# Query/key norms through 32-column sums and one inverse root, and VectorE operations over two PSUM banks

## What is computed

```python
q = _causal_dwconv_silu(q_l + qd, q_conv_w).reshape(b, s, h, dh)
k = _causal_dwconv_silu(k_l + kd, k_conv_w).reshape(b, s, h, dh)
...
q, k = (_l2norm(q), _l2norm(k))     # x * rsqrt(sum(x * x) + 1e-6) over the 16 channels of a head
...
Sd = gt[..., None, None] * Sst                       # per token: decay the state,
kS = jnp.einsum('bhk,bhkv->bhv', kt, Sd)             # read it with the key,
Snew = Sd + jnp.einsum('bhk,bhv->bhkv', kt, bt[..., None] * (vt - kS))
ot = jnp.einsum('bhk,bhkv->bhv', qt, Snew)           # and again with the query
...
scores = jnp.einsum('bhqd,bhkd->bhqk', q * SCALE, k) # cross attention: softmax over 64 keys
```

## Time and profile before

| | us |
|---|---|
| time of three runs | median 1374.06 (1372.43 to 1379.7) |
| the profiled execution: its own time | 1380.29 |
| its span in the trace | 1378.5 |
| turn i = 0 / steady turns i = 1 to 6 / drain and last | from 47 / some 155 each from 202 on / from about 1120 and 1267 |

### The profile page before, as it was taken

One profiled execution on the slowest core, in us unless ns is written; L12 is line 12 of the kernel. 1 busy time (PEld: TensorE's weight loads), 2 busy tenths in 40 slices (PEclk: granted clock), 3 DMA queues, 4 the chain that ended last, 5 costly groups with the idle time before them and its releaser, 6 DMA issues.

```text
span 1378.5 us, 40816 instructions
## 1 busy us (share of the span) xinstructions
PE 1291.2 (94%) x17045; PEld 838.7 (61%) x17077; DVE 1139.6 (83%) x3060; ACT 907.6 (66%) x1760; POOL 206.8 (15%) x204
## 2 busy tenths in 40 slices
...
PEclk9999999999999999999999999999999999999999
...
DMA packets 22782, 35.77 MB, mean 26 GB/s; under 512 B 1992, under 2 KB 18504, under 8 KB 22344
## 3 DMA queue, kind: packets, MB, share of 16 engines
...
## 4 chain that ended last, share of the span: by engine, by line
PE 68%; DVE 16%; ACT 10%; issue 4%; DMA 1%; POOL 0%; SPq 0%; DVEq 0%; ACTq 0%
PE bank L2210 14%; PE four L1970 5%; PE bank L1884 5%; PE bank L1757 4%; PE bank L1782 4%; PE bank L2125 4%; PE bank L2103 3%; PE bank L2139 3%; PE four L1989 2%; PE four L1782 2%; PE bank L1886 2%; ACT L833 2%; PE bank L1811 2%; PE four L2014 2%; PE bank L1789 2%
## 5 line engine op out<-in xcount | busy, mean ns | idle before, releaser
L2210 PE MATMUL bank<-w_sb,cs 128*128 128x512 f32 x512 | 248.7, 602 | 2.9 <-ACT qkv L1109 0.4
L798 POOL TENSOR_TENSOR decayed<-state,pk 128x512 f32<-128x512 f32 x64 | 76.1, 1189 | 671.3 <-DVE state L1499 671.3
L2210 PEld LDWEIGHTS bank<-w_sb,cs 128*128 128x128 f32 x512 | 92.4, 189 | 95.8 <-issue 71.5
L1109 ACT ACTIVATE cs<-bank 128x512 f32<-128x512 f32 x112 | 66.9, 598 | 99.2 <-PE bank L1763 48.8
L833 ACT ACT_TABLE_LOAD x82 | 105.2, 1283 | 1.5
L1357 DVE SCALAR_TENSOR_TENSOR qkv<-pre,l_sb,qkv 128x512 f32<-128x512 f32 x144 | 101.6, 751 | 0.0
L1884 PE MATMUL bank<-hT,w_sb 128*128 128x512 f32 x192 | 95.2, 619 | 3.9 <-ACT hid L913 2.2
L1696 DVE SCALAR_TENSOR_TENSOR cs<-cs,rwt 128x256 f32<-128x256 f32 x196 | 88.2, 485 | 6.2 <-ACT cs L1109 2.8
L1045 ACT COPY cs<-bank 128x512 f32<-128x512 f32 x114 | 66.0, 579 | 41.3 <-PE bank L2125 41.2
L1582 DVE TENSOR_REDUCE pkc<-bank 128x8 f32<-128x512 f32 x116 | 74.3, 682 | 21.1 <-PE bank L2103 20.0
L1811 PEld LDWEIGHTS bank<-c_sb 128*128 128x128 f32 x588 | 74.6, 199 | 11.3 <-issue 10.3
...
## 6 DMA issues: line engine op xcount, KB each, us to landing
...
```

The source lines that it names most:

```text
L798: fin("dec", tt(decayed[:, :, :, :], state[:, :, :, :], eGC[:, c, :].unsqueeze(1).unsqueeze(3).to_broadcast([P, 4, G * B, DH]), ALU.mult))
L2210: mm(dst, x1T[:, k, b * TB:b * TB + TB], ew[:, k, ep * 512:ep * 512 + 512], start=k == 0, stop=False)
```

## The change

The norms: the four blocks of squares are kept in four buffers. One step `sum` makes four products with 32-column weights (`bones8`), each of which fills 32 partitions of the one bank 0, with eight head sums in four copies. One `rs` takes Ln and Exp over 128 x 512. A new step `rsp` spreads the roots by four products of 32 rows each (`wide8`) into banks 0 to 3; it waits for `rs`, and, since it overwrites what `grow` left, for `d_ready` (behind `gsub.1`) and both `egr` (behind `gexp.1` and `gexp.2`, which now wait for `d_ready` themselves). `norm` reads its factor from PSUM. `vturn` waits for two norms. On VectorE the paired operations of `max`, `zc`, `dsel`, `gsub`, the tap copies and the halo copies become one operation each over both halves, and `psub` is one signal a unit. All lists and the `KEEP` table are new. Cut to its core (the order lists are shown where the text speaks of them):

```diff
-DVE_IN, DVE_AB, DVE_CD, ACT_IN, ACT_AB, ACT_CD = 22, 64, 57, 2, 6, 18
+DVE_IN, DVE_AB, DVE_CD, ACT_IN, ACT_AB, ACT_CD = 19, 62, 49, 2, 3, 18
...
     "steady": {
         "pe": steps('''
+        -router.0 +gate.1 grow -turn2.0 sum +cond -qx.0.0 rsp -turn2.1 -qx.0.1 vturn -qx.1.0 -sc.0.0 -sc.0.1 -qx.1.1
+        raw.0 raw.1 -sc.1.0 -sc.1.1 -pt.0 raw.2 -pt.1 raw.3 raw.4 -pv.0 raw.5 raw.6 -pt.2 -sc.2.0 -sc.2.1 -pt.3 raw.7
...
+        cs.7.0 cs.7.1 -turn6.1 *rot co.0 co.1 -ffd.0 -ffd.1 onorm.0 *gate.0 onorm.1 wo.0 -ffu.0 -ffu.1 wo.1 wo.2'''),
         "dve": steps('''
+        -ln2.0.0 -ln2.0.1 dsel.0 dsel.1 gsub.0 gsub.1 -ln2.1.0 -ln2.1.1 norm.0 norm.1 norm.2.0 norm.3.0 norm.2.1
+        norm.3.1 -max.0.0 -max.0.1 -max.1.0 am.0 +cond -max.1.1 am.1 -av.0.0 am.2 -av.0.1 -max.2.0 -max.2.1 am.3
...
         "act": steps('''
+        sq.2 -moe.0 -moe.4 -ln2.0 -moe.18 +cond.0 sq.3 -turn2.0 +gate.1 rs gexp.2 gexp.1 -ln2.1 gexp.0 -turn2.1 -qx.0
...
     "drain": {
         "pe": steps('''
+        +proj.1.0 grow +proj.1.1 -turn2.0 -turn2.1 -qx.0.0 -qx.0.1 sum -qx.1.0 rsp -qx.1.1 -sc.0.0 vturn -sc.0.1 raw.0
...
         "act": steps('''
+        +proj.4 -ln2.0 -ln2.1 sq.2 -turn2.0 sq.3 -moe.14 -turn2.1 -qx.0 gexp.1 kx.0 gexp.2 -top.0 -route.0 *gate.0 rs
...
 # first(i), ScalarE
-                    if j >= 2:
-                        up("sum_ps", j - 1)
-                    fin("sq", A(osq[:, j % 2, :], qkv[:, j, :], ACT.Square))
+                    fin("sq", A(squares[j], qkv[:, j, :], ACT.Square))
+                def sum_():
                     log_exp()
+                    up("sum_ps")
+                    inv_sqrt(ch, squares[0], bank[0][:, :], eps6, 1.0, "rs")
...
                     else:
+                        up("d_ready")
                         g = k - 1
                         fin("egr", A(egr[:, 32 * g:32 * g + 32, :].rearrange("p n t -> p (n t)"), bank[2 + g][:, :], ACT.Exp))
...
 # first(i), VectorE
-                        for a, n in enumerate(pair):
-                            tap[a] = ch1.link(V.tensor_copy(pre[:, n % 4, :, 0:3], halo[:, n, :, :]))
+                        at = 2 * m % 4
+                        tap[0] = tap[1] = ch1.link(V.tensor_copy(pre[:, at:at + 2, :, 0:3], halo[:, 2 * m:2 * m + 2, :, :]))
...
-                        up("rs", j + 1)
-                    tmp = norms[:, 32 * (j % 2):32 * (j % 2) + 32, :]
+                        up("rsp_ps")
+                    tmp = v3(bank[j][:, :])
...
+                    ring = flat(zc_ring[:, c % 4, :, :, :].rearrange("p n x m -> p n (x m)")).rearrange("p (a n) -> p a n", a=2)
+                    fin("zc", stt(ring, four[:, 2:4, 0:D], C("x0"), C("zx").unsqueeze(1).to_broadcast([P, 2, D]), ALU.mult, ALU.add))
...
 # second(j), VectorE
-                        for a in range(2):
-                            up("sc_ps", 2 * u + a + 1)
-                            highest[a] = link(red(mx[:, a, :], sc[a], AX.X, ALU.max))
+                        up("sc_ps", 2 * u + 2)
+                        highest[0] = link(red(flat(mx), sc, AX.X, ALU.max))
...
+                    fin("psub", tt(prob_of(j, u).rearrange("p (h n) -> p h n", h=16), sc, bc(flat(mx), NK), ALU.subtract))
...
 # first(i), TensorE
-                    fin("sum_ps", mm(bank[j % 2][:, :], C("bones"), osq[:, j % 2, :], start=True, stop=True))
+                def sum_():
+                    up("sq", 4)
+                    if i:
+                        pe.wait_ge(ev["ors"].sem, ev["ors"].at(i - 1, 2))
+                    tiled()
+                    for j in range(4):
+                        last = mm(bank[0][32 * j:32 * j + 32, :], C("bones8"), squares[j], start=True, stop=True)
+                    fin("sum_ps", last)
+                def rsp():
+                    up("rs")
+                    up("d_ready")
+                    up("egr", 2)
+                    tiled()
+                    for j in range(4):
+                        rows_ = slice(32 * j, 32 * j + 32)
+                        last = mm(bank[j][:, :], C("wide8")[rows_, :], squares[0][rows_, :], start=True, stop=True)
+                    fin("rsp_ps", last)
                 def vturn():
                     up("bv")
-                    up("rs", 4)
+                    up("qk_norm", 2)
...
-                    up("psub", 2 * (u - depth) + 1 + a) if u >= depth else up("qx_sb")
+                    up("psub", u - depth + 1) if u >= depth else up("qx_sb")
```

More of the change, by code:

```diff
@@ L117 @@
         "pe": steps('''
[L118 to L127, removed]
@@ L177 @@
-        cs.7.0 cs.7.1 *rot -pv.5 -ffd.1 -mo.1.0 -moe.11 -pt.5 co.0 -ffd.0 co.1 -moe.25 onorm.0 wo.0 -pt.4 -pt.11 -pt.9
-        onorm.1 *gate.0 +sum.0 -pt.10 wo.1 -moe.28 -sc.1.0 -moe.0 -sc.7.1 -mo.0.0 wo.2 -mo.0.1 -qx.0.0 -ffu.1 -sc.5.1
-        -moe.18 +sum.1'''),
-        "dve": steps('''
-        -av.3.1 norm.0 dsel.0 -acc.1.1 norm.1 dsel.1 -max.3.1 -av.4.1 gsub.0 -av.3.0 norm.2.0 norm.3.0 gsub.1 -acc.4.1
-        norm.2.1 -acc.10.1 -max.2.0 -acc.7.1 norm.3.1 am.0 am.1 -max.7.1 -max.2.1 am.2 +cond am.3 solve.0.0 solve.0.1
@@ L209 @@
-        -ln2.0 +rs.0 -moe.27 -pt.9 -hnorm.0 -ffd.1 +rs.1'''),
+        -moe.11 -wp.0.0 -turn2.1 -sc.2.0 -turn5.1 +gate.1 grow -sc.1.1 -pt.2 -wp.0.1 sum +cond -moe.2 rsp -moe.8
+        -pw.1.0 vturn -sc.4.0 -moe.15 -moe.21 raw.0 -moe.26 -pv.6 raw.1 raw.2 -pt.1 raw.3 -pt.0 -moe.5 -pt.3 -mi raw.4
+        -pw.1.1 -rturn.0 -sc.2.1 -moe.29 raw.5 -moe.7 -pt.10 raw.6 raw.7 +db +proj.0.0 -moe.30 +proj.0.1 -turn4.0 +btr
+        +brep.0 +proj.1.0 +proj.1.1 -pt.7 d1.0 -asum.1 -pt.13 -moe.1 -sc.3.0 +brep.1 -moe.6 -turn6.0 -moe.27 -moe.24
```

507 lines of the change are left out of this document (247 added, 260 removed).

## The result

Four runs of the changed kernel took 1401.64 to 1409.46 us, median 1406.16; before, the median was 1374.1. The ratio is 1.0224, with a 95% interval of 1.018 to 1.0268. The forecast was 1403, in a range of 1367 to 1419. The profiled execution is the fastest of the four (1401.64, span 1399.8).

A forecast was written before the change was run, and what follows sets the result against it. The prediction took nearly all of a turn as TensorE's work in order, with VectorE nearly full and equally late in C. Steady 24, head 1.8, drain 3.9 and last -1.0 made +28.7 us on 1374.1, about 1403, range 1367 to 1419.

The forecast's parts named there:

- C: Part of a steady turn from `wo.1` to the next `raw.0`; forecast 2.2 us longer.
- TensorE's products: Four `sum` products, 3.44 us a turn, go; tiled `sum` 0.9 and `rsp` 1.0 come; the 3.44 reappear as waits.
- B: Part of a steady turn from `rot` to `wo.1`, 11.4 us; forecast to get no shorter when `sum.0` leaves it.
- The merges: Paired VectorE operations made one, all in A: forecast gain of 1.0 us a turn, between a 0.5 loss and 2.5.
- A: Part of a steady turn from `raw.0` to `rot`, 126.1 us; forecast 125, wrong if it shrinks by more than 2.
- The clock: TensorE falls to half clock behind the 3.3 us hole ahead of `rsp`: one low stretch, 2.8 us a turn.
- granted clock under 1.00 in each steady turn: Sign to be seen in the new trace: TensorE's clock below its high level in every steady turn, its length about 159.
- Head: Turn ahead of the steady ones: `raw.0` at 92.45 where it came about 90.65, +1.8 us.
- drain: Turn behind the steady ones: `raw.0` at t + 17.3, +2.9 us, and 1.0 for a low clock, 3.9 in all.
- last: The last part of the run, with 16 merges: -1.0 us.
- t: End of `wo.2`, from which times in C are counted; steady `raw.0` forecast at t + 16.2, before t + 14.0.
- The sum: Steady 6 x (2.2 - 1.0 + 2.8) = 24, head 1.8, drain 3.9, last -1.0: +28.7 us.

The follow-up runs named there:

- `early_egr`: Changed kernel with the exponents of banks 2 and 3, and through them `rsp`, waiting for the first decay subtraction, not the second; 1397.56 us, ratio 1.018.
- `refit`: Changed kernel with exponents behind `gsub.0`, second layer norm earlier, `rsp` in two halves, two query norms between them, ScalarE and TensorE lists reordered; 1385.61 us, ratio 1.009.
- `refit_spread`: `refit` with GpSimd's spreading copy of the decays moved behind `dec.7` in the steady turns; 1386.52 us, ratio 1.010.
- `fill_hole`: Changed kernel with 12 products without use ahead of `rsp` in the six steady turns; 1398.35 us, ratio 1.019.
- `merges_only`: Kernel before, its lists and norms kept, with only the merged VectorE operations of the change; 1372.09 us, ratio 0.999.

## Why the prediction was right

**Direction and cause hold, and so does the size, in part by luck (see the sum)**: the six norms that now wait for `rsp`, and through it for `gsub.1` and both `egr`, make C longer. C of the kernel before at 17.7 against 20.5 after, at high clock in both, is +2.8 a turn; I had +2.2. The 0.6 between is TensorE's row behind `rsp`: I said 5.1 us would just cover the norms; it took 5.7 (992.96 to 998.62), and ended 0.5 us behind the keys' spread. The experiments that shortened what stands ahead of the norms (`early_egr`), took norms out of the row, and reordered what is queued behind (`refit`) brought C down to 18.2. By the whole turn they gave back 1.1 us (`refit`) and 1.5 (`refit_spread`) of 2.7.

**TensorE's products**: `sum` in four tiles took 1.06 us to its end and `rsp` 1.07 to the next start, for the 0.9 and 1.0 taken, so the four tiles do overlap, and the loss is not in them. The 3.44 us taken out reappear as waits: 1.8 ahead of `wo.1` with B unchanged at 11.45, and 2.7 ahead of `rsp`.

**The merges** were a term that failed: -1.0 us a turn, and A and B together became 0.3 shorter (824.4 us after 826.2 over the six steady turns). Even that is not theirs: the sixth turn alone became 2.1 shorter, and there the kernel before had a low clock from 1106.1 to 1113.0 (granted 0.51) and the changed one none; the other five together became 0.3 longer. Part of the reason is shown: alone they free 2 us of VectorE a turn and gain 0.3, so A is in the main TensorE's own row; in the changed kernel what they free is spent again, in part on the collision with GpSimd that the new lists brought (A 0.4 shorter without it).

**The clock** was sized wrong: one low stretch in each steady turn at 2.8 us each, 16.8 in all; the profile had them in four of six, costing 1.3, 2.7, 1.3 and 1.3, together 6.7. `fill_hole` puts it at 7.8 on the median. So the sign "granted clock under 1.00 in each steady turn" did not come true in two of the six. By the page "TensorE: Matmul & The Clock Gate", Part 1, in the Trainium skill, the engine falls to the lower level behind idle time; the runs agree, with the limit that the same wait of 2.69 us went with it in some turns and not in others.

**Head, drain, last.** Drain: C is 4.1 longer at high clock, where 3.9 was forecast with 1.0 of clock in it. `rsp` began at t + 11.5, as forecast (11.4), but 0.9 of the surplus is a term left out: the new `KEEP` table puts six products without use ahead of this `raw.0` (before three), and they ran from 1155.29 to 1156.83, while the keys were spread at 1155.91. From the drain's `raw.0` to the end: -0.4 for -1.0. Head: `raw.0` came 5.3 us later for 1.8 (95.97 after 90.65; the low stretch fell on it from 86 on), but the head's last `wo.1` came 3.8 earlier (180.49 after 184.25): the kernel before had two more low stretches there, at 126 to 133 and 157 to 164. The longer C of turn 1 used this up (`raw.0` at 202.33 after 202.22).

**The sum** came right because the errors have opposite signs: C 16.8 for 13.2 and A 4 us less gain than said, against 10 us less of clock. That they cancel is luck. In the profiled execution the stretch from the first steady `raw.0` to the drain's, with five steady C and the drain's, took 954.5 us after 932.9: +21.6, where 5 x (2.2 + 2.8) - 6 x 1.0 + 3.9 = 22.9 was forecast. Its whole is +21.3 on the profiled one of before, which was itself 6 above its median; median against median it is +32. The two profiled executions had nearly the same granted clock over the span (0.989 and 0.990). The four of the changed kernel had 0.990 (1401.64), 0.987 (1403.87 and 1408.45) and 0.984 (1409.46), while 17 later ones of the kernel before had 0.991 to 0.999. So it is likely, though no profile of such an execution shows it, that most of the 10.7 us between +21.3 and +32 is low clock too, and that the clock is worth more in a typical execution than the profile's 6.7.

**What stays open.** With the dependence and the orders repaired the time is still 1385.6 us, 11 above the kernel before on the same chip: some 1.2 to 1.6 us of each turn, 2.7 of the drain turn (C of 20.9 against 18.1) and the clock in head and drain and in one steady turn. Whether the norms or the new lists cost these is not shown. The wait of 1.8 us ahead of `wo.1` was in all kernels with the new lists (`merges_only`, with the old ones, has none in the steady turns), and it is the largest wait left in a turn of `refit`; nothing that depends on `rsp` can fill it, and no experiment tried to. No version beat the kernel before clearly; `merges_only` comes nearest, at 0.999.
